# Head of a fused RWKV and attention kernel: token sums by products, half-width projections, first scores from 512 tokens

## The reference, cut to what matters

```python
pooled = hidden_states.mean(axis=1)              # hidden_states = xn
logits = relu(pooled @ gw1.T + gb1) @ gw2.T + gb2
gates  = softmax(top_k(logits, 2))
q = _svd_moe(xn, qWm, qU, qS, qV, qb, idx, gates) * SCALE   # x@W.T + sum_k gate_k*(x@V*S)@U.T + b
k, v = the same with their own weights
attn = softmax(q @ k.T per head);  out = _svd_moe(attn @ v, oWm, ...)
```

## Time and profile before

| what | us |
|---|---|
| median of 3 runs (451.94, 449.52, 449.80) | 449.80 |
| the profiled execution, its time | 448.59 |
| its span, first to last instruction | 446.9 |
| PE busy in that span | 421.5 (94%) |
| DVE busy | 368.6 (82%) |
| ACT busy | 345.2 (77%) |
| POOL busy | 191.0 (43%) |

### The profile page before, as it was taken

How to read it: one execution, slowest core, us unless ns; L and a number is a source line. 1 busy time by engine, 2 the same in 40 slices (tenths; PEclk the granted TensorE clock), 3 DMA queues, 4 the chain that set the end, 5 groups by cost and what they waited for, 6 DMA issues and landing times.

```text
span 446.9 us, 8497 instructions
## 1 busy us (share of the span) xinstructions
PE 421.5 (94%) x3223; PEld 144.1 (32%) x3224; DVE 368.6 (82%) x649; ACT 345.2 (77%) x469; POOL 191.0 (43%) x270
## 2 busy tenths in 40 slices
PE   1889989999999999999999999999999999999993
PEld 1644223333232223232323223323332333322153
DVE  8578899998999997899999789999888999950023
ACT  3547837879887898788799969778986877987862
POOL 5029581935551525282353646416265611321200
PEclk9988999999999999999999999999999999999998
DMA  7004303141414141405141413342422421010314
GB/s 240 11 11 56 39 5 34 20 66 21 63 23 67 20 65 19 63 7 72 23 64 20 66 13 57 29 62 24 61 24 26 59 50 13 26 12 27 95 58 155
DMA packets 45661, 20.84 MB, mean 47 GB/s; under 512 B 36788, under 2 KB 36916, under 8 KB 45620
## 3 DMA queue, kind: packets, MB, share of 16 engines
q1 hardware_dynamic: 44782, 19.60, 27.7%
q10 hardware_dynamic: 838, 0.69, 0.5%
HBM read 4.88 MB, written 5.24 MB: 23 GB/s over the span
## 4 chain that ended last, share of the span: by engine, by line
PE 84%; DVE 9%; ACT 3%; DMA 2%; issue 1%; SPq 0%; DVEq 0%
PE banks L1411 26%; PE banks L1398 22%; PE banks L1321 18%; PE banks L1366 8%; DVE half_max L1134 5%; PE banks L1283 3%; ACT probs L950 3%; PE banks L1289 1%; DMA parts<-ctx_dram 1%; PE banks L1267 1%; PE banks L1218 1%; PE banks L1454 1%; PE banks L1275 1%; PE banks L1184 1%; DVE stats L1002 1%
## 5 line engine op out<-in xcount | busy, mean ns | idle before, releaser
L1134 DVE TENSOR_REDUCE half_max<-banks 128x1 f32<-128x512 f32 x512 | 318.6, 683 | 21.2 <-PE banks L1321 19.6
L950 ACT ACTIVATE probs<-banks 128x1024 f32<-128x1024 f32 x256 | 248.2, 1023 | 47.8 <-PE banks L1398 44.6
L1411 PE MATMUL banks<-probs,v_op 128*32 128x512 f32 x1024 | 136.4, 605 | 0.6 <-ACT probs L950 0.6
L1321 PE MATMUL banks<-k_main,q_main 64*128 64x512 bf16 x512 | 117.6, 388 | 5.6 <-DVE half_max L1134 3.3
L1398 PE MATMUL banks<-q_main,k_main 64*128 64x512 bf16 x512 | 99.3, 377 | 0.4 <-ACT probs L950 0.2
L1398 PE MATMUL banks<-q_tail,k_tail 35*128 35x512 bf16 x512 | 99.3, 377 | 0.0
L1321 PEld LDWEIGHTS banks<-k_main,q_main 64*128 64x128 bf16 x512 | 36.5, 93 | 151.0 <-DVE half_max L1134 132.2
L1398 PEld LDWEIGHTS banks<-q_tail,k_tail 35*128 35x128 bf16 x512 | 27.2, 94 | 25.9
L1398 PEld LDWEIGHTS banks<-q_main,k_main 64*128 64x128 bf16 x512 | 26.4, 95 | 27.0 <-ACT probs L950 12.5
L1411 PEld LDWEIGHTS banks<-probs,v_op 128*32 128x32 f32 x1024 | 20.1, 108 | 32.7 <-issue 30.3
L696 POOL TENSOR_TENSOR work<-work 128x512 f32<-128x512 f32 x16 | 16.6, 1039 | 28.6 <-ACT work L939 28.6
(11 more groups left out here) (177 smaller groups left out, 413.7 us busy)
## 6 DMA issues: line engine op xcount, KB each, us to landing
ctx_dram<-ctx_sb SPq DMA_DIRECT2D x16, 256.0 KB, 2.0
q_main<-parts SPq DMA_DIRECT2D x60, 48.0 KB
k_main<-parts SPq DMA_DIRECT2D x60, 48.0 KB
parts<-ctx_dram SPq DMA_DIRECT2D x8, 256.0 KB, 4.0
mat_sb<-in_mats_dram SPq DMA_DIRECT2D x2, 768.0 KB, 5.2
v_op<-V SPq DMA_DIRECT2D x16, 64.0 KB, 3.8
out_dram<-x_sb SPq DMA_DIRECT2D x4, 256.0 KB, 3.1
q_main<-parts SPq DMA_DIRECT2D x30, 32.0 KB
```

The source lines that it names most:

```text
L950: a.activation(probs[:, (2 * step + h) % 4, :, :], banks[:, 2 * h:2 * h + 2, :], ACT.Exp).then_inc(b_read, 1)
L1134: v.tensor_reduce(half_max[:, n % 2, u:u + 1], ring_bank(at), axis=AX.X, op=ALU.max).then_inc(a_read, 1)
L1321: mm(dst, q_main[HALF * e:HALF * (e + 1), s, P * c:P * c + P], k_main[HALF * e:HALF * (e + 1), s, CHUNK * h:CHUNK * h + CHUNK], start=True ...
L1411: last = mm(banks[g:g + 32, PV_BANK, :], v_op[:, s % 2, step, e, :], probs[:, (2 * step + h) % 4, e, :], start=(step == 0), stop=True, ski ...
```

## The change

- **Normalisation.** DVE normalises chunks 0 and 2, POOL chunks 1 and 3.
- **Token sums.** They no longer come from ACT's copies but from PE: for each chunk four float32 products with a block of xn as stationary operand and two columns of `mean_w` (1/128) as moving operand, accumulated in bank 4. DVE copies the two sums to SBUF. One gate product instead of two, with the scale 128/T.
- **Order of transposes.** Chunk 0, sums 0 and 1, chunk 1, sums 2 and 3; chunks 2 and 3 are transposed after the second gate product, in place of 24 of the 32 idle products.
- **row_of** is written by POOL instead of ACT.
- **U scaling.** DVE scales only q and k of batch 0; POOL scales the other six. `expert_weights` and `add_main` of q and k are done for batch 0 first (128 columns), those of batch 1 later.
- **Projections.** q of chunk 0 and k of chunk 0 first, split and laid out first; k of chunk 1 next; q of chunk 1, the last part of k of chunk 1 and both their layouts move into the opening, between places 2 and 9. The first place waits for the rows in banks 0 and 2 only; place 8 for bank 3, place 16 for bank 1. The first 16 places take chunk 0 of the queries first.
- **Opening.** New `FILL_JOBS`; turn_h(0) ahead of the first place; late projections 0 and 1 before the RWKV products; ACT's queue mixes the remaining parts and layouts with its old work.
- **SP** issues the rows of pair 1 before the tails of pair 0.

```diff
-FILL_JOBS = {2: [("turn", 0), ("turn", 1)], 5: [("turn", 2), ("turn", 3)], 9: [("values", 0)], 12: [("values", 1)]}
-FILL_JOBS.update({15 + 2 * m: [("mixed", m)] for m in range(6)})
-FILL_JOBS.update({26: [("late", 0)], 28: [("late", 1)], 30: [("late", 2)], 31: [("late", 3)]})
+FILL_JOBS = {2: [("left", 3, 1), ("project", 1)], 3: [("turn", 1)], 4: [("rows", 3)], 5: [("left", 1, 0)],
+             7: [("left", 1, 1)], 9: [("rows", 1)], 10: [("turn", 2)], 11: [("turn", 3)],
+             12: [("values", 0)], 14: [("values", 1)], 16: [("late", 0)], 18: [("late", 1)], 20: [("mixed", 0)],
+             22: [("mixed", 1)], 24: [("mixed", 2)], 26: [("late", 2)], 27: [("late", 3)],
+             29: [("mixed", 3)], 31: [("mixed", 4)], 33: [("mixed", 5)]}
...
-            load_tails(0, 0)
             load_pair(1, 1)
+            load_tails(0, 0)
...
+            def normalise(n):
+                for i in range(4 * n, 4 * n + 4):
+                    g.tensor_scalar(xn_tok[:, i, :], x_sb[:, i, :], moments[:, i, 0:1], rstd[:, i:i + 1],
+                                    ALU.subtract, ALU.mult).then_inc(xn_in[1], 1)
             for b in range(B):
+                normalise(2 * b + 1)
...
+            for i, b in ((2, 0), (2, 1), (3, 0), (3, 1), (0, 1), (1, 1)):
+                g.tensor_scalar(u_s[:, i, b, :], mat("qkvo"[i] + "U"), sg[:, i, b:b + 1], None, ALU.mult
+                                ).then_inc(us_ready, 1)
...
-            keep_h(0)
-            keep_h(1)
-            scale_shift(0)
-            keep_h(2)
-            keep_h(3)
-            scale_shift(1)
+            part(0, 0, 0)
+            part(0, 0, 1)
+            part(0, 0, 2)
+            part(3, 0, 0)
+            keep_rows(0)
+            part(3, 0, 1)
+            keep_h(0)
+            part(3, 0, 2)
+            part(1, 0, 0)
+            keep_h(1)
+            keep_rows(3)
+            part(1, 0, 1)
+            scale_shift(0)
+            part(1, 0, 2)
+            keep_rows(1)
+            keep_h(2)
+            scale_shift(1)
+            keep_h(3)
...
+            def sum_tokens(n):
+                b = n // 2
+                pe.wait_ge(xn_in[n % 2], 4 * (n // 2 + 1))
+                for k in range(CHUNK // P):
+                    last = mm(banks[:, 4, 32 + 2 * b:34 + 2 * b], xn_tok[:, 4 * n + k, :], mean_w[:, 0:2],
+                              start=(n % 2 == 0 and k == 0), stop=(n % 2 == 1 and k == 3))
+                return last
...
+            turn_x(0)
...
+            sum_tokens(0)
+            sum_tokens(1)
+            turn_x(1)
...
+            sum_tokens(2)
+            sum_tokens(3).then_inc(sums_ps, 1)
+            warm(4)
...
-            warm(8)
+            warm(6)
...
-            warm(32)
+            turn_x(2)
+            turn_x(3)
+            warm(8)
...
             project(0)
-            project(1)
             pe.wait_ge(weff_ready, 2)
             project(2)
             take_part(0, 0)
...
+            expert_weights(2, None, weff_ps)
+            expert_weights(3, None, weff_ps)
+            take_part(2, 0)
+            take_part(0, 1)
...
             project(3)
...
+            take_part(2, 1)
...
+            pair_rows(0)
...
+            expert_weights(0, 1, weff_ps)
+            expert_weights(1, 1, weff_ps)
             take_part(3, 0)
+            pair_rows(2)
...
+            turn_h(0)
```

More of the change, by code:

```diff
@@ L269, in build @@
         left_ps = [sem(f"left_ps{j}") for j in range(CHUNKS)]
+        rows_kept = [sem("rows_kept"), sem("k_row_kept")]
+        xn_in = [sem(f"xn_in{n}") for n in range(2)]
         part_ready = [sem(f"part_ready{j}") for j in range(CHUNKS)]
@@ L776, in keep_xnT @@
                 act.wait_ge(x_transposed, n + 1)
-                a.activation(columns_of(xnT, n), bank(n), ACT.Copy, accum_out=sums[:, n:n + 1]).then_inc(xnT_ready, 1)
-            for n in range(CHUNKS):
-                keep_xnT(n)
+                a.copy(columns_of(xnT, n), bank(n)).then_inc(xnT_ready, 1)
+            keep_xnT(0)
+            keep_xnT(1)
             act.wait_ge(gate_h_ps, 1)
@@ L790, in _ @@
             a.activation(rstd2[:, :], rstd2[:, :], ACT.Exp, scale=-0.5).then_inc(rstd2_ready, B)
[L791 to L803, removed]
+            keep_xnT(3)
             act.wait_ge(qb_ready, 2)
@@ L812, in part, with keep_rows @@
                              bias=col("kb") if t else qb_s[:, 0:1]).then_inc(part_ready[j], 1)
[L814 to L821, removed]
+            def keep_rows(j):
+                t, n = part_bank(j, 0)
+                act.wait_ge(rows_ps, ROW_ORDER.index(j) + 1)
+                a.copy((k_main if t else q_main)[:, 0, CHUNK * n:CHUNK * (n + 1)], bank(j)).then_inc(rows_kept[0], 1)
             def keep_h(u):
@@ L887, in _ @@
             keep_gate(1)
-            for j in range(CHUNKS):
-                keep_late(j)
             copy_turned(0)
@@ L1206, in _, with expert_weights @@
             warm(12)
-            def expert_weights(i):
-                at, half = WEFF_AT[i]
-                pe.wait_ge(us_ready, 2 * i + 2)
-                mm(bank(at)[:, B * P * half:B * P * (half + 1)], mat("qkvo"[i] + "V"),
-                   u_s[:, i, :, :].rearrange("p b o -> p (b o)"), start=True, stop=True).then_inc(weff_ps, 1)
+            def expert_weights(i, b, done):
+                at, quarter = WEFF_AT[i, b]
+                width = B if b is None else 1
+                mm(bank(at)[:, P * quarter:P * (quarter + width)], mat("qkvo"[i] + "V"),
+                   (u_s[:, i, :, :] if b is None else u_s[:, i, b:b + 1, :]).rearrange("p b o -> p (b o)"),
+                   start=True, stop=True).then_inc(done, 1)
             def project(j):
@@ L1225, in take_part, with pair_rows @@
                    skip_group_check=True).then_inc(left_ps[j], 1)
+            def pair_rows(j):
+                t, n = part_bank(j, 0)
+                pe.wait_ge(part_ready[j], PARTS)
+                for i in range(PARTS):
+                    last = mm(bank(j), row_of[:, t, i, :], parts[0:2 * HD, t, i, n, :], start=(i == 0),
+                              stop=(i == PARTS - 1))
+                last.then_inc(rows_ps, 1)
             pe.wait_ge(moe_in, 16)
-            expert_weights(0)
-            expert_weights(1)
+            for i in range(2):
+                pe.wait_ge(us_first, i + 1)
+                expert_weights(i, 0, weff_ps)
             warm(4)
+            pe.wait_ge(xnT_ready, 1)
             pe.wait_ge(weff_ready, 1)
             project(0)
-            project(1)
             pe.wait_ge(weff_ready, 2)
@@ L1288, in project_late @@
                 bank_free(f"late{j}")
+                pe.wait_ge(weff_ready, 6)
+                pe.wait_ge(xnT_ready, CHUNKS)
                 mm(bank(fill_bank(f"late{j}")), w_eff[:, t, 1, :], columns_of(xnT, n), start=True, stop=True
                    ).then_inc(late_ps, 1)
[L1292 to L1304 removed]
             pe.wait_ge(weff_ready, 4)
+            turn_h(0)
             pe.wait_ge(keys_set, 1)
@@ L1337, in between @@
                     turn_max(0)
-                for what, of in FILL_JOBS.get(at, ()):
+                for what, of, *which in FILL_JOBS.get(at, ()):
                     if what == "turn":
                         turn_h(of)
+                    elif what == "left":
+                        take_part(of, *which)
+                    elif what == "project":
+                        project(of)
+                    elif what == "rows":
+                        pair_rows(of)
                     elif what == "values":
```

181 lines of the change are left out of this document (96 added, 85 removed).

## The result

The changed kernel took 454.75 us in the median of 4 runs (453.94 to 455.33), the kernel before in the same session 449.66 (449.32 to 451.94): ratio 1.0104, 95% interval 1.0081 to 1.0127. It is slower by 1%, where no change that can be measured was forecast, and outside the range. All ratios are taken over the fast executions of both kernels, without those more than 1.5% above the fastest of their own kernel, and are not the quotients of the medians beside them.

The account below looks back on a forecast made before the run. PE and DVE fill the main loop, so head and opening changes pass to the end; the head is a chain, the opening PE's, then DVE's. -2.7 + 1.8 = -0.9 gave 448.9 us from 449.8, range 446.8 to 452.6.

Parts of the forecast that it names:

- Token sums: Head, PE: 16 instruction pairs per group at 0.12 each at full clock, at most twice that at half; gate product 1.8 later.
- d: Delay of the gate products against 14.25 us in the old trace; taken as 1.8.
- the slow rival: Head: clock stays at half through the sums, d = 4.35, gate chain 0.4 more; 451.9 to 453.6 us, chance 0.20.
- Gate chain: Head: DVE part unchanged, transposes and eight fills (0.5) fit; first projection 5.25, first place 13.35 after the gate product.
- the halved expert step: Head: two 128-column products and two half-width additions (0.24); first projection starts at 19.5 instead of 20.1.
- Opening: Opening: bank 1's late part makes PE wait 1.9 and DVE idle 1.6; place 15 at 40.1 against 41.78.
- a rival of 0.10 and 3.2: Opening: PE's wait for bank 1 makes the clock fall, costing up to 3.2; 452.1 us, chance 0.10.
- -2.7 at d = 0: Opening: ends 2.7 us sooner than before if the gate products are not delayed.
- Normalisation: Head: POOL takes 0.3 an instruction (bounds 0.19 and 0.77), chunks ready before PE needs them; price nothing.
- The rival in which POOL and DVE exclude each other: Head, normalisation: both slowed to the sum, chunk 0 ready 1.0 later; 449.9 us, chance 0.07.
- POOL's scaling of U: Head: six scalings at 0.3 each from 18.3, done near 20.1; price nothing.
- Main loop and SP: Main loop untouched, passing earlier changes on one for one; SP starts at 35.2 instead of 28.19, covered by about 2 us.

Follow-up runs that it names:

- e3: Changed kernel with 54 fill products ahead of the first transpose, product sums and POOL's normalisation kept: 455.91 us, ratio 1.0108.
- e7: Changed kernel with DVE normalising all, sums still products, 54 fills ahead of the first transpose and 24 before bank 1's layout: 447.88 us, ratio 0.9964.
- e10: Changed kernel with DVE normalising all, sums from ACT's copies, 54 fills ahead, 20, 4, 4, 8 after the chunks, 24 before bank 1's layout: 445.62 us, ratio 0.9902.
- e1: Changed kernel with the third part of bank 1 moved ahead of scale_shift(0) on ACT: 452.74 us, ratio 1.0073 to the kernel before.
- e2: Changed kernel with 24 unread fill products on PE ahead of bank 1's layout: 450.59 us, ratio 1.0008 to the kernel before.
- e4: Changed kernel with token sums back on ACT's copies, DVE normalising all, four chunks transposed in a row: 453.66 us, ratio 1.0073.
- e15: Kernel before, order untouched, with e10's head fills and 16 fills between the layouts and the first place: 450.19 us, ratio 0.9967.
- e9: Changed kernel with 24 fills before bank 1's layout and DVE normalising all four chunks: 450.71 us, ratio 1.0027.
- e5: Kernel before with 16 fill products between the four layouts and the first place: 450.28 us, ratio 1.0002.
- e8: Changed kernel with bank 1's third part ahead of scale_shift(0) on ACT and 8 fills in the remaining wait: 451.28 us, ratio 1.0047.
- e16: The kernel of e10 measured again, beside e15 on one chip: 446.12 us, ratio 0.993.
- e13: Same kernel as e15, measured earlier: 448.63 us, ratio 0.9951; its profiled execution took 1015.69 us.

## Why the prediction was wrong

Its sum at the opening end was -0.9; it was +6.1. By its steps:

**Token sums: the step that failed first.** The price 0.12 at full clock was right (e3, e7), and at half clock the measured 0.21 lies within the bound of 0.24. What failed is the choice of case: "The new order has no gap in PE between 9.2 and 10.2, so the clock could rise a little sooner than it did; I take d = 1.8". It rose only after 20.7, behind all the sums and eight transposes more: d was 3.4. That was the slow rival, whose argument (products of few columns stand where transposes had stood) was on the page with 0.20, and e7 points the same way from the other side. The rival's own d of 4.35 was too high, since 0.21 and not 0.24 is the price.

**Gate chain and the head behind it.** First projection 5.25 after the gate product: 6.2. About 0.5 of that is the gates' broadcast (line 1243), 3.83 after the gate product where it was 3.34, because eight fills ran at half clock (0.85 in the chain, not 0.5) behind transposes at half clock. Another 0.35 is the halved expert step: from its first product to the first projection it is 1.01, in e10 at full clock too, where the sum had 0.66 and the kernel before 1.32. First place 13.35 after the gate product: 14.19, and 13.39 in e10, so that this forecast holds where the clock does. Against 16.66 before, the new head saved 2.5 of the 3.3 foretold.

**Opening: the wait was right, its price was not.** ACT's part behind scale_shift, PE waiting 1.9 and DVE idle 1.6 were foretold; the rows have 1.70 and 2.37. The sum charged only the wait. It took the clock fall as a rival of 0.10 and 3.2; it came in the wait for bank 1, where the rival had it, lasted from 39.2 to 49.4, and cost 4.2. e1 puts a limit on the rival's reason: with the wait down to 0.46 the clock fell as well. By its own test ("if PEclk shows 0.50 between 28 and 50") the prediction falls here. And both rivals came together, which no case had: the late head and the fall are 1.9 and 4.2. Each alone was measured inside or near the range of 446.8 to 452.6: e2, the late head without the fall, 450.59; e4, the fall without the late sums, 453.66.

**-2.7 at d = 0** was near in size: without late sums and without falls (e10) the opening ends 2.55 before 66.88. That closeness is in part luck, since e10 has fills that the change had not, and the reason was half wrong. The working took the old times as the price of the old order, and these held a stretch at half clock, 30.9 to 37. e15 gets 1.7 of the 2.55 in the old order by fills alone.

**Normalisation** was mis-sized: 0.83 an instruction, where 0.3 was taken between 0.19 and 0.77, so even the upper bound was too low. It was hidden, as said (e9), but only because the sums were late: e3, with sums at full clock, waited for it. The rival in which POOL and DVE exclude each other is not borne out: GpSimd took 0.83 with and without DVE beside it, DVE's own instructions had a median of 344 ns here and 337 before, and chunk 0's transposes started at 8.30 and not 1.0 later than 8.23. POOL's scaling of U also took about twice the estimate, 3.56 for six:

```profile
22.44 3.56 POOL L572 TENSOR_SCALAR u_s<-mat_sb,sg 128x128 f32<-128x128 f32 x6 [5.62 <-DVEq L1083]
```

It cost no wait: the products at 26.19 in the chain (line 1251) need the first four, done at 24.83, and those at 29.37 the last two, done at 26.00.

**Main loop and SP** were right: the loop is as busy as before, and the rest after the opening end is 380.6 against 380.0. SP started at 39.59, right behind the late last part, and spent 9.0 on the twelve DMAs of pair 1; between 45 and 75 the profile puts PE's waits down to DVE alone.

## What to carry to other kernels

Before PE is given work to save another engine or to fill a wait, ask what clock it will run at and whether that work keeps the clock: 16 float32 products of two columns (32 records) made the gate product 3.4 late here; as a by-product of ACT's copies the same sums had delayed nothing. Price a new wait on PE twice, once as the wait and once as a stretch at half clock behind it, and test the second with fill products in the gap before reordering anything. When durations of the old trace are carried over, first take out those that ran at half clock, or a gain that a few fill products would bring is put down to the new order. And look at the whole span after each fill: a fall that is gone in one place was seen again in another.

## What the hardware showed beyond what was expected

- A busy PE is not enough for its clock. In e7 PE had no gap from 10.26, and the clock fell at 13.0 among float32 products with two moving columns; in the changed kernel the durations stay those of half clock from 8.30 to 20.7, through sums, transposes and fills. In e5 PE was unbroken from 30 to 35 and ran partly at 0.50, after layouts with 16 rows. Which property of this work keeps the clock down, no run here isolates.
- The Trainium skill, TensorE: Matmul & The Clock Gate, What's actually happening, says that activity releases the throttle. The 54 fills of e3 and e10 agree: the four transposes after them take 0.66 where they took 1.09. By the item above it does not foretell the changed kernel, where PE was at work from 8.30 to 20.7 at half clock.
- The granted clock reads 1.00 for 9.2 to 17.4 in the changed kernel while durations are those of half clock. In the head the durations say more than that column.
- A fall put right in one place can come back in another: e5 from 30 to 58, e8 from 40 to 67, and e16, the kernel of e10, had one at 64 in its profiled execution that e10's had not. Near the end of the span every profile but e13's has one (the kernel before, the changed one and e10 alike), and its length varies from run to run.
- GpSimd's operation with two scalars per partition took 0.83 for 128 x 128 float32 where DVE needs 0.26; with one scalar per partition it took 0.59 (six in 3.56).
